# Three engines' instruction orders in a fused attention block: where ScalarE issues its moves, where VectorE transposes, and what it does between

## The reference, cut to what matters

```python
h = _layernorm(x, ln1_g, ln1_b)
x = _attention(h, h, sa_wq, sa_wk, sa_wv, sa_wo, sa_bo) + x
h = _layernorm(x, ln2_g, ln2_b)
x = _attention(h, cond_emb, ca_wq, ca_wk, ca_wv, ca_wo, ca_bo) + x
h = _layernorm(x, ln3_g, ln3_b)
p = h @ ff_w1 + ff_b1
a, gate = (p[..., :D_FF], p[..., D_FF:])
h = a * jax.nn.gelu(gate, approximate=False) @ ff_w2 + ff_b2
return h + x
```

## Time and profile before

| what | value |
|---|---|
| time, median of 3 runs | 3368.15 us (3367.66 to 3375.95) |
| the profiled execution's own time | 3373.26 us, span 3371.4 us |
| TensorE matmul (PE) busy | 3018.8 us, 90% of the span |
| TensorE weight load (PEld) busy | 2610.7 us, 77% |
| VectorE (DVE) busy | 2236.8 us, 66% |
| ScalarE (ACT) busy | 1842.3 us, 55% |
| GpSimd (POOL) busy | 1537.7 us, 46% |
| DMA engines | 44 to 46% busy in passes 1 and 2 |
| mean granted PE clock | 0.973 of full speed |

### The profile page before, as it was taken

How to read it: one execution, slowest core, us unless ns; L and a number is a source line. 1 busy time by engine, 2 the same in 40 slices (tenths; PEclk the granted TensorE clock), 3 DMA queues, 4 the chain that set the end, 5 groups by cost and what they waited for, 6 DMA issues and landing times.

```text
span 3371.4 us, 77077 instructions
## 1 busy us (share of the span) xinstructions
PE 3018.8 (90%) x25600; PEld 2610.7 (77%) x25600; DVE 2236.8 (66%) x3433; ACT 1842.3 (55%) x5903; POOL 1537.7 (46%) x1385
## 2 busy tenths in 40 slices
PE   5999999999999999788888888888888889999999
PEld 4777777777777777577777777777777768999999
DVE  5777777777777777667777777777777764444444
ACT  4555555555555555456555555555566653333333
POOL 2444444444444444244444444444444443544454
PEclk8999999999999999999999999999999999999999
DMA  6444444444444444444444444444444441111111
GB/s 164 117 118 118 118 118 118 117 117 117 116 118 118 118 118 118 123 118 125 125 123 125 123 123 124 123 123 124 124 125 125 125 121 48 41 43 47 47 41 40
DMA packets 423997, 365.12 MB, mean 108 GB/s; under 512 B 74640, under 2 KB 422160, under 8 KB 423696
## 3 DMA queue, kind: packets, MB, share of 16 engines
q1 hardware_dynamic: 345104, 297.39, 32.6%
q10 hardware_dynamic: 78848, 67.16, 7.5%
HBM read 70.66 MB, written 25.17 MB: 28 GB/s over the span
## 4 chain that ended last, share of the span: by engine, by line
issue 44%; POOL 31%; DVE 10%; PE 7%; ACT 5%; POOLq 1%; ACTq 1%; SPq 0%; DMA 0%; DVEq 0%
POOL probs L904 17%; PE unit_ps L417 6%; ACT probs L596 4%; POOL a_lo L943 4%; POOL x_rb L898 3%; DVE neg_max L744 3%; DVE blocks L757 3%; POOL hT_lo L910 2%; POOL rstd L890 2%; DVE hT L738 2%; DVE x_out L787 1%; PE s_ps L417 1%; POOL hT_hi L917 1%; POOL hT_lo L913 1%; POOL ln_shift L892 1%
## 5 line engine op out<-in xcount | busy, mean ns | idle before, releaser
L904 POOL TENSOR_TENSOR probs<-probs,row_inv 128x1024 f32<-128x1024 f32 x512 | 970.2, 1895 | 1300.4 <-DVE row_inv L749 1300.4
L596 ACT ACTIVATE probs<-s_ps,neg_max 128x256 f32<-128x256 f32 x2048 | 951.3, 489 | 791.2 <-DVE neg_max L744 763.3
L417 PE MATMUL unit_ps<-hT_hi,w_hi 128*128 128x256 f32 x2048 | 609.2, 300 | 181.1 <-DVE x_out L787 139.8
L757 DVE STREAM_TRANSPOSE blocks<-probs 128x1024 f32<-128x1024 f32 x512 | 635.8, 1242 | 71.9 <-POOL probs L904 71.8
L744 DVE TENSOR_REDUCE neg_max<-s_ps 128x4 f32<-128x1024 f32 x512 | 596.1, 1202 | 20.1 <-PE s_ps L431 19.9
L417 PE MATMUL unit_ps<-hT_hi,w_lo 128*128 128x256 f32 x2048 | 582.8, 290 | 0.0
L417 PEld LDWEIGHTS unit_ps<-hT_hi,w_hi 128*128 128x128 f32 x2048 | 410.7, 201 | 218.4 <-DVE x_out L787 154.9
L417 PE MATMUL unit_ps<-hT_lo,w_hi 128*128 128x256 f32 x1792 | 518.7, 289 | 0.0
L768 DVE TENSOR_TENSOR qk_lo<-unit_ps,qk_hi 128x512 fp32r<-128x512 f32 x512 | 344.1, 672 | 261.0 <-ACT qk_hi L633 261.0
L443 PE MATMUL o_ps<-pT,v_f 128*64 128x256 f32 x4096 | 502.0, 387 | 15.9 <-DVE a_lo L763 11.4
L596 ACT ACTIVATION_READ_ACCUMULATOR probs<-s_ps,neg_max 128x1 f32 x2048 | 449.0, 219 | 0.0
(11 more groups left out here) (62 smaller groups left out, 6044.5 us busy)
## 6 DMA issues: line engine op xcount, KB each, us to landing
pT<-blocks SPq DMA_DIRECT2D x3328, 64.0 KB, 2.0
pT<-blocks ACTq DMA_DIRECT2D x768, 64.0 KB, 2.1
x_res<-in_x_dram SPq DMA_DIRECT2D x32, 256.0 KB, 2.7
x_sa_dram<-x_out SPq DMA_DIRECT2D x32, 256.0 KB, 2.3
x_ln<-x_sa_dram ACTq DMA_DIRECT2D x32, 256.0 KB, 3.2
ctx_in<-in_ctx_dram SPq DMA_DIRECT2D x32, 256.0 KB, 3.2
x_res<-x_sa_dram SPq DMA_DIRECT2D x32, 256.0 KB, 2.8
x_ca_dram<-x_out SPq DMA_DIRECT2D x32, 256.0 KB, 2.4
```

Source lines behind the costliest of these rows:

```text
L417: last = nc.tensor.matmul(dst, a, b, start=start and n == 0, stop=stop and n == len(terms) - 1)
L596: op = nc.scalar.activation(probs[:, m % 2, r, :], s_ps[:, m % 2, r // IT, r % IT * S:(r % IT + 1) * S], ACT.Exp, bias=neg_max[:, m % RING ...
L757: nc.vector.transpose(blocks[:, n % 2, m % 2, :, :].rearrange("p b (j r c) -> p r j b c", j=IT, c=BLK), probs[:, m % 2, :, :].rearrange("p ...
L904: nc.gpsimd.tensor_tensor(probs[:, m % 2, :, :], probs[:, m % 2, :, :], row_inv[:, m % RING, :].unsqueeze(2).broadcast_to([P, ROWS, S]), A ...
```

## The change

It reorders instructions; none is added or removed, and the two attention passes alone are touched.

- ScalarE: `move_blocks` goes from behind `attended_hi` at the head of a step to the end of the step, behind the last unit copied (and the norm or `split_inputs`).
- VectorE: the second transpose of a step, `transpose_blocks(2n+1)`, goes to the next step, between its first and its second `maxima`. The first transpose goes behind the second `qk_remainders`.
- VectorE: `attended_lo` and `norm_statistics` go behind the first `qk_remainders`; `scale_inputs` goes behind the first `invert_sums`; `project_out(t-1, 0)` goes from step 2 to the end of step 1.

```diff
--- before.py
+++ after.py
@@ -651,8 +651,6 @@
                             split_weight(k)
                         if behind := attended_before(t, n, parts):
                             attended_hi(*behind)
-                        if ready := moved(t, n, parts):
-                            move_blocks(*ready)
                         if "cur" in parts:
                             exponentials(t, 2 * n)
                         for k in splits(ph, n, parts):
@@ -671,6 +669,8 @@
                             normalise(*norm)
                         if n == 2 and "nxt" in parts and parts != FILL:
                             split_inputs(t + 1)
+                        if ready := moved(t, n, parts):
+                            move_blocks(*ready)
                         for k in splits_after(ph, n, parts):
                             if n == 0:
 
@@ -801,32 +801,32 @@
                             dve.wait_ge(norm[0].bn_done, norm[1] + 1)
                         if "cur" in parts:
                             maxima(t, 2 * n)
+                        if behind := moved(t, n, parts):
+                            transpose_blocks(behind[0], 2 * behind[1] + 1)
+                        if "cur" in parts:
                             maxima(t, 2 * n + 1)
                         if n == 1 and norm:
                             norm_moments(*norm)
-                        if behind := attended_before(t, n, parts):
-                            attended_lo(*behind)
-                        if n == 2 and "nxt" in parts:
-                            scale_inputs(t + 1)
-                        if n == 2 and "prv" in parts:
-                            project_out(t - 1, 0)
-                        if n == 0 and norm:
-                            norm_statistics(*norm)
                         for k in splits(ph, n, parts):
                             split_weight(k)
                         if "cur" in parts:
                             invert_sums(t, 2 * n)
+                        if n == 2 and "nxt" in parts:
+                            scale_inputs(t + 1)
                         for pair in pairs[:1]:
                             qk_remainders(*pair)
+                        if behind := attended_before(t, n, parts):
+                            attended_lo(*behind)
+                        if n == 0 and norm:
+                            norm_statistics(*norm)
                         if "cur" in parts:
                             invert_sums(t, 2 * n + 1)
-                            transpose_blocks(t, 2 * n)
                         for pair in pairs[1:]:
                             qk_remainders(*pair)
                         if "cur" in parts:
-                            transpose_blocks(t, 2 * n + 1)
-                        if n == 3 and "prv" in parts:
-                            project_out(t - 1, 1)
+                            transpose_blocks(t, 2 * n)
+                        if n % 2 and "prv" in parts:
+                            project_out(t - 1, n // 2)
                         for k in splits_after(ph, n, parts):
                             split_weight(k)
                 over_batches(dve, B, iteration, first=2)
```

## The result

The changed kernel takes 3056.7 us (median of 4 runs, 3051.6 to 3058.3) against 3370.4 us before: a ratio of 0.9065, 95% interval 0.9048 to 0.9081, some 314 us faster. The forecast was 3088. TensorE's mean granted clock rose from 0.973 to 0.991, and its busy share from 90% to 96% of a shorter span.

The account below looks back on a forecast made before the run. TensorE was taken as the bound, held in the attention passes by waits on other engines' orders. Thirty batches per pass saving 135 and 145 us, 280 together, took 3373.3 to 3093, or 3088 as median; whole range 3045 to 3190.

Parts of the forecast that it names:

- TensorE's own work: TensorE's time per batch with waits taken out: 37.9 us in pass 1, 36.3 in pass 2.
- the ends of the passes: The two end iterations of each attention pass, counted as gaining nothing.
- 2.2 us wait for line 787: Step 2: qk6 waits 2.16 us for the wo0 bank; moving project_out(t-1, 0) earlier removes it, 3 us to spare.
- waits for `qk_lo`: TensorE's waits for the qk remainders, 0.49 and 0.69 us in the batch shown, go with qk_lo(3) 1.0 us early.
- The walk's times: Pass 1 event times after T, the start of a step's scores: first maximum at 1.0 us, exponentials at 2.4.
- The wait that stays in pass 2: Step 2: GpSimd's remainders end at 12.1 us, TensorE wants them at 10.8; 1.35 us of waiting per batch stays.
- The rival in which the shortfall stays: Both attention passes: TensorE's clock stays low for as long as now, 76 us more, 3164 us; chance 0.12.
- New waits: Rival: a new wait of about 1.2 us in two steps of a batch, 144 us more, 3232; chance 0.08.
- thin places: v's copy before qk7, attended_lo before attend, ScalarE's moves running into the next exponentials: 0 to 0.8 us to spare.
- ScalarE's moves: Every step: block moves run 8.1 to 10.1 us after the scores start, over the step's border; attended_hi comes at 10.7.
- The cover: ScalarE's spare time before the next step's exponentials: 1 us; in step 2, 0.5 in pass 1, about nothing in pass 2.
- SyncE's queue: Block-move issues, 35.5 us of a 37.9 us batch: holds with 2.4 us. Rival: becomes the slower bound, 3550; chance 0.05.

Follow-up runs that it names:

- act_only: Kernel before, with only ScalarE's block moves put at the end of the step: 3276.2 us, ratio 0.9712.
- proj_only: Kernel before, with only project_out(t-1, 0) moved from step 2 to the end of step 1: 3248.5 us, ratio 0.9629.
- proj_undone: Changed kernel, with project_out(t-1, 0) put back in step 2, behind scale_inputs: 3278.3 us, ratio 0.9720.
- tr_undone: Changed kernel, with both transposes back at their old places: 3107.4 us, ratio 0.9223.
- dve_only: Changed kernel, with ScalarE's moves back at the head of the step: 3892.3 us, ratio 1.1515.
- by_act4: Changed kernel, with a fourth move a step issued on ScalarE's queue: 3051.0 us, ratio 0.9053.
- ctx_dve: Changed kernel, with TensorE's context wait split and one context remainder on VectorE instead of GpSimd: 3047.2 us, ratio 0.9048.
- alo_undone: Changed kernel, with attended_lo and norm_statistics back ahead of invert_sums and the first qk_remainders: 3057.8 us, ratio 0.9075.

## Why the prediction was right

The time lies in the forecast's range, 31 us below its point. The mechanism was right; what was off are sizes, and the largest two, TensorE's own work and the ends of the passes, err the same way.

- **Which waits go.** Right: the 2.2 us wait for line 787 and the waits for `qk_lo` went in every steady batch, and `act_only`, `proj_only` and `proj_undone` show that they have separate causes: the moves' place for most of `qk_lo`, `project_out`'s place for line 787.
- **The walk's times.** Exponentials 2.4 us after T: 2.28 to 2.37 measured. First maximum 1.0: 1.02. `qk_lo` of step 1 done at 7.8: 7.8 (497.69 + 0.69 - 490.58). The wait that stays in pass 2, 1.35 us: 1.29.
- **TensorE's own work.** The term was mis-sized, 37.9 us for pass 1 and 36.3 for pass 2, where it is 37.49 and 35.9 (37.20 less the wait of 1.29). I took the waits in brackets off the old steps. A bracket counts from the end that the profile gives the matmul before it, but in a full stream the next one starts ahead of that end: `attend` is given as 1.95 us and the scores start 1.88 us after its start (488.70 to 490.58); the four matmuls of the x unit are given as 0.60 us and `qk6` starts 0.35 after their start (502.97 to 503.32). A wait costs this overlap as well. So step 0 is 9.21, not 9.27, step 1 is 9.27, not 9.35, and step 2 is 9.74, not 9.90. For step 3 the rows had the right number, 9.27 without a wait (999.98 to 1009.25), where I put 9.35. Over 30 batches and two passes this gives 24 us, and the shorter wait, the rounding up to 37.7 and a shorter last batch of each pass bring it to some 29. (The "42.1" for the batch shown was misread too: from 1009.25 to 1050.84 it is 41.6. Nothing rests on it.)
- **What the batches and the ends brought.** Thirty batches of pass 1 went from 1271.6 us (118.28 to 1389.86) to 1123.4 (106.01 to 1229.44), thirty of pass 2 from 1269.2 (1506.62 to 2775.86) to 1115.4 (1338.39 to 2453.80): 302 us, where the sum had 280. The window that I used for pass 2 before was 0.24 us a batch dearer than its mean, which takes 7 off the 29. The ends, counted at nothing without a reason, gave 13: 12 before the first full batch and 8 between the passes, less 7 behind pass 2. Together 35 us between the profiled executions. The changed kernel's profiled execution stands only 1.6 us above its median, not 5.1, so 31 between the medians.
- **The clock.** Right that it returns: 1.00 in the windows of both passes, though TensorE waits 1.29 us in each batch of pass 2. The rival in which the shortfall stays is out. By estimate it was worth 0.027 x 3371 - 0.009 x 3056 = 64 us of the 314. The remark that 257 of the 280 us are idle time does not fit this, for it leaves 23 for the clock and the restarts; the mis-sized work had taken up the difference.
- **New waits.** The thin places were named rightly: v's copy ahead of `qk7` is what `proj_only`, `tr_undone` and `dve_only` run into, and `attended_lo` in `dve_only`. In the changed kernel TensorE waits at none of them in a steady batch.
- **ScalarE's moves.** Right for steps 0 and 2, wrong for 1 and 3. In step 0 they run 7.6 to 9.7 us after T (488.94 to 491.09), where I had 8.1 to 10.1, over the border at 490.58, and `attended_hi` behind them starts 0.70 us after the next T instead of 0.12. The cover held: ScalarE is still idle for 1.06 us ahead of the exponentials of 492.93. In steps 1 and 3 they are issued before the computing instructions ahead of them are done, in step 3 from 1.6 us before the last copy starts (514.32, against 515.96), and the border is not reached. That step of the walk was wrong in the safe direction. A fourth move (`by_act4`) costs nothing either.
- **SyncE's queue.** Right that it holds at 0.64 us an issue; that it would be the next bound could be seen in the sum (35.5 of 37.9), but I did not draw on it: `ctx_dve` ran into it.
- **`attended_lo`.** Right that its place costs nothing (`alo_undone`).

What I had not said is how much the parts depend on one another. Without ScalarE's part, VectorE's is worth minus 519 us. With all the rest in place, the transposes' new places bring 51 us and `project_out`'s 222, against 125 alone.

## What to carry to other kernels

- Before a queue's order is changed, walk one step with the instruction offsets of every engine and write down, for each thing that the bound engine waits for, by how much it is early. The thin places of such a walk are where the next edit fails.
- A wait that is taken away gives room only as far as the next source allows. An instruction that waits for a late result and that nothing on its own engine needs, such as a DMA issue on a computing engine, belongs where its result has long been there. At the head of a step it holds everything behind it (`dve_only`).
- When two bounds lie side by side, removing one at a time shows little: `ctx_dve` and `by_act4` brought 9 and 6 us, and together 43.

## What the runs showed of the hardware

- DMA issues on ScalarE's queue go on beside its computing: in step 3 of the changed kernel above, the first of three issues comes while exponentials run that stand ahead of it in program order. How early it comes fits the results that the instructions ahead of it wait for, not their execution: the unit that the last copy empties leaves TensorE at 514.21 (513.93 + 0.28) in step 3 and at 488.77 (488.37 + 0.40) in step 0, and the first issues come at 514.32 and 488.94. No run was made to test this reading. In the kernel before, where the exponentials stood behind the issues, they started only when these were over (1022.81 behind 1022.71).
- A move costs its queue 0.64 us (8.30 for 13, in `ctx_dve`), and 13 a step fill SyncE's. The Trainium skill ("DMA: Bandwidth & Descriptors", Issuing engines are not separate DMA queues) says that issuing from several engines saves only the sequencer's issue time, usually small against the DMA. Here it was not small: with 2.0 us from issue to landing and 52 issues a batch it became the bound of pass 2.
- In `ctx_dve` the subtraction of 128x256 took 1.43 us on VectorE, though one of 128x512 with one operand in PSUM takes 0.69. GpSimd's line in the same stretch stands behind it:

```profile
1737.44 1.43 DVE L768 TENSOR_TENSOR hT_lo<-ctx_in,hT_hi 128x256 fp32r<-128x256 f32 x1
```

```profile
1737.31 1.28 POOL L917 TENSOR_TENSOR hT_lo<-hT,hT_hi 128x512 fp32r<-128x512 f32 x1
```

GpSimd reads from 1737.31 to 1738.59, and VectorE, begun at 1737.44, ends at 1738.87, 0.28 us after it. The Trainium skill ("SBUF — State Buffer", Who interferes with whom) says that a VectorE instruction with two SBUF inputs and a GpSimd instruction that reads SBUF block one another, the later one in full. The trace agrees, and the 29 batches behind 1350 us show the same (1.42 to 1.44 us each); no run here had that subtraction with GpSimd idle.
- The granted clock fell to the 1.2 GHz level behind many waits of TensorE of 1.8 to 2.4 us, but not behind all (34 of 60 in the steady batches of the kernel before), and behind none of the 1.29 us waits of the changed kernel's pass 2 nor of `proj_only`'s waits for v's copy of 0.8 to 1.65 us.
